# One 2-byte tile per slot of a fused feed-forward stage, turned by a transposing transfer and not by TensorE

## What is computed

```
x = x + tanh(g_xattn[0]) * L0_xattn(layernorm(x), ctx, Wq, Wk, Wv, Wo)
x = x + tanh(g_ffn[0]) * L0_ffn(layernorm(x), weight_scales, weight_q)      # bf16 x bf16
x = x + tanh(g_xattn[1]) * L1_xattn(layernorm(x), ctx, Wq, bq, Wk, bk)
x = x + tanh(g_ffn[1]) * L1_ffn(layernorm(x), W, b, A, B, gate_w, gate_b)

def L0_ffn(x, scales, q):
    w = dequantize(q, scales).astype(bfloat16)
    return einsum('bsi,oi->bso', x.astype(bfloat16), w)
```

## Time and profile before

| | |
|---|---|
| time, median of 3 runs | 1989.47 us (1989.45 to 1989.71) |
| the profiled execution's own time | 1992.98 us |
| its span, from the first to the last instruction | 1991.2 us |
| PE busy | 1956.6 us (98%) |
| DVE, ACT, POOL busy | 1037.7, 742.4, 724.0 us |
| TensorE clock granted, mean | 0.993 of full speed |
| HBM traffic | 177.01 MB read, 57.94 MB written, 118 GB/s |

### The profile page before, as it was taken

One profiled execution on the slowest core, in us unless ns is written; L12 is line 12 of the kernel. 1 busy time (PEld: TensorE's weight loads), 2 busy tenths in 40 slices (PEclk: granted clock), 3 DMA queues, 4 the chain that ended last, 5 costly groups with the idle time before them and its releaser, 6 DMA issues.

```text
span 1991.2 us, 37538 instructions
## 1 busy us (share of the span) xinstructions
PE 1956.6 (98%) x14016; PEld 1298.5 (65%) x14030; DVE 1037.7 (52%) x2012; ACT 742.4 (37%) x1560; POOL 724.0 (36%) x719
## 2 busy tenths in 40 slices
PE   8999999999999999999999999999999999999998
PEld 3488888885666666666666655667566676666665
DVE  5655545534555555555555663434334345656554
ACT  5421111222555555555555661111111224444441
POOL 0000000111565566565555550101101246666662
PEclk9999999999999999999999999999999999999999
DMA  7433333333222222223322444433333485665661
GB/s 249 132 99 109 96 109 100 121 97 81 67 69 68 66 69 66 66 69 81 98 72 66 115 121 140 116 92 115 114 113 111 141 274 166 208 214 185 210 208 58
DMA packets 317583, 236.43 MB, mean 119 GB/s; under 512 B 248270, under 2 KB 285134, under 8 KB 313004
## 3 DMA queue, kind: packets, MB, share of 16 engines
q1 hardware_dynamic: 290364, 222.47, 38.3%
q10 hardware_dynamic: 27120, 12.60, 2.4%
HBM read 177.01 MB, written 57.94 MB: 118 GB/s over the span
## 4 chain that ended last, share of the span: by engine, by line
PE 88%; DVE 3%; ACT 2%; DMA 1%; issue 1%; POOL 0%; SPq 0%; DVEq 0%; ACTq 0%
PE a_pr L723 14%; PE b_kv_ps L1137 9%; PE b_kv_ps L1141 9%; PE c_x_ps L1609 9%; PE d_f_ps L2050 8%; PE b_s_ps L1178 8%; PE b_o_ps L1193 7%; PE c_t_ps L1630 7%; PE d_a_ps L1835 3%; PE a_pr L719 3%; PE b_mx_ps L1153 3%; PE c_f_ps L1662 2%; PE d_s_ps L1803 2%; DMA t_scratch<-c_tT 1%; PE c_x_ps L1204 1%; DVE d_y3T L2005 1%
## 5 line engine op out<-in xcount | busy, mean ns | idle before, releaser
L937 POOL TENSOR_TENSOR b_probT<-b_exp,b_probT 128x448 f16<-128x448 f32 (+2 forms) x256 | 265.3, 1038 | 297.2 <-ACT b_probT L1001 297.1
L503 POOL TENSOR_TENSOR cT<-ctx_raw,cT 128x375 f16<-128x375 f32 x256 | 222.4, 888 | 134.6 <-ACT cT L498 133.6
L723 PE MATMUL a_pr<-a_yT,proj_q_p 128*128 128x256 f16 x2016 | 223.2, 273 | 0.0
L723 PEld LDWEIGHTS a_pr<-a_yT,proj_q_p 128*128 128x128 f16 x2016 | 197.3, 98 | 23.4
L1141 PE MATMUL b_kv_ps<-wkv_p,cT 128*128 128x384 f16 (+1 forms) x1152 | 210.6, 325 | 0.0
L1071 DVE TENSOR_REDUCE b_nmax<-b_mx_ps 112x2 f16<-112x974 f32 x128 | 149.6, 1169 | 109.6 <-PE b_mx_ps L1153 109.5
L1137 PE MATMUL b_kv_ps<-cT,wkv_p 128*128 128x375 f16 x1152 | 198.9, 323 | 0.0
L1178 PE MATMUL b_s_ps<-b_qT,b_kT 96*128 96x448 f16 (+5 forms) x768 | 190.6, 356 | 2.2 <-DMA b_qT<-b_nrow 2.2
L1193 PE MATMUL b_o_ps<-b_probT,b_v 128*128 128x448 f16 (+5 forms) x768 | 187.3, 351 | 0.0
L999 ACT ACTIVATE b_exp<-b_s_ps 128x448 f32<-128x448 f32 (+2 forms) x256 | 137.7, 538 | 129.7 <-PE b_s_ps L1178 124.4
L2050 PE MATMUL d_f_ps<-wo_early,d_y3T 128*112 128x512 f16 x768 | 175.7, 382 | 0.0
(11 more groups left out here) (209 smaller groups left out, 2797.8 us busy)
## 6 DMA issues: line engine op xcount, KB each, us to landing
ctx_raw<-in_ctx_t SPq DMA_DIRECT2D x32, 1500.0 KB, 7.4
d_cn_raw<-in_ctx_nat SPq DMA_DIRECT2D x32, 512.0 KB
b_qT<-qk_scratch SPq DMA_DIRECT2D x32, 336.0 KB, 4.1
o_scratch<-b_o SPq DMA_DIRECT2D x128, 84.0 KB, 2.0
qk_scratch<-a_heads SPq DMA_DIRECT2D x70, 144.0 KB, 2.1
d_cn_raw<-in_ctx_nat SPq DMA_DIRECT2D x16, 476.0 KB
x_scratch<-c_x SPq DMA_DIRECT2D x14, 512.5 KB, 3.5
tiles_in<-in_x SPq DMA_DIRECT2D x14, 512.0 KB, 4.0
```

Of the source, the lines that this page charges most:

```text
L503: pool.tensor_tensor(cT[:, p, 1, k, 0:S], ctx_raw[:, k, :], cT[:, p, 0, k, 0:S], ALU.subtract).then_inc(split_lo, 1)
L723: last = mm(pr[:, n % PR, 0:GT * P], w[:, b, k, at * P:(at + 1) * P], yT[:, g % 2, a, k, :], start=(x == 0 and k == 0), stop=(x == 2 and k ...
L937: pool.tensor_tensor(pT[0:m, c, 1, :], ex[0:m, i % 2, :], pT[0:m, c, 0, :], ALU.subtract).then_inc(p_lo, 1)
```

## The change

Turning `y1` leaves TensorE. SP issues one transposing transfer per tile, SBUF to SBUF, from `y1` to `y1T`. PE's eight transposes and ACT's copy are gone; PE waits for the transfer before the feed-forward product, and DVE waits for the transfer of the tile before, where it waited for PE's transposes. SP's wait and issue (`turn_y1`) stand at the start of slot s, ahead of `load`, for tile s-1. SP's slots are all written out, none is in a loop; the other engines keep their loops.

```diff
+                    def turn_y1(t):
+
+                        sp.wait_ge(y1_ready, t + 1)
+                        wait(sp, f_done, 2 * t)
+                        sp.dma_start(y1T.rearrange("p (k r) -> p k r", k=KD), y1[:, :], transpose=True
+                                     ).then_inc(y1_turned, 16)
+
                     def slot(j, p, s):
+                        if inside(s - 1, TILES):
+                            turn_y1(s - 1)
                         if inside(s, TILES) and inside(s + 1, TILES) and not (isinstance(s, int) and s == 0):
                             load(j + p, 1 - p, s + 1)
...
-                    run_slots(sp, slot, SLOTS, 4)
+                    for s in range(SLOTS):
+                        slot(s // 2, s % 2, s)
...
-                        if inside(s - 1, TILES):
-                            act.wait_ge(y1tr, s)
-                            act.activation(y1T[:, :], tr[:, 0, :].bitcast(BF16), ACT.Copy).then_inc(y1T_ready, 1)
...
                         if inside(s, TILES):
-                            wait(dve, y1tr, s)
+                            wait(dve, y1_turned, 16 * s)
                             norm1_scaled(dve, y1[:, :], x1[:, p, :], P, s).then_inc(y1_ready, 1)
...
-                        if inside(s - 1, TILES):
-                            pe.wait_ge(y1_ready, s)
-                            for k in range(KD):
-                                last = pe.transpose(tr[:, 0, k * P:(k + 1) * P].bitcast(BF16), y1[:, k * P:(k + 1) * P],
-                                                    identb[:, :])
-                            last.then_inc(y1tr, 1)
...
                         if inside(s - 1, TILES):
-                            pe.wait_ge(y1T_ready, s)
+                            pe.wait_ge(y1_turned, 16 * s)
```

More of the change, by code:

```diff
@@ L1357, in build @@
                 wo_done, x1_ready = sem("c_wo_done"), sem("c_x1_ready")
-                y1_ready, y1tr, y1T_ready = sem("c_y1_ready"), sem("c_y1tr"), sem("c_y1T_ready")
+                y1_ready, y1_turned = sem("c_y1_ready"), sem("c_y1_turned")
                 f_done, f_read, x2_ready = sem("c_f_done"), sem("c_f_read"), sem("c_x2_ready")
```

## The result

The changed kernel takes 2009.35 us, the median of three runs (2004.42 to 2009.95), against 1989.47 us before. The ratio is 1.0093, with a 95% interval of 1.0079 to 1.0107: slower by 0.9%. The profiled execution took 2009.35 us with a span of 2007.6 us, 16.4 us more than the 1991.2 of before. The forecast was 2007.5 us, and +18.0 us on the span.

A forecast was written before the change was run, and what follows sets the result against it. PE, busy for 98% of the span, was taken to bound the kernel. The terms -5.4 + 2.2 + 0.5 + 24.9 - 7.2 + 3.0 = +18.0 us on 1989.5 gave 2007.5 us, range 1999 to 2026 us.

The forecast's parts named there:

- Steady slots: Slots 2 to 13 of stage c: PE is freed of 0.45 us of transposes in each, 5.4 us gained.
- The transfer's price: Time of one transposing transfer in a steady slot, taken as 5 us, within 13.9 us of room.
- The 18.6 us of the other row: High bound for one transposing transfer, from the dearest row per KB, 84 KB in 6.1 us.
- Slot 1: First tile: the transfer lands behind the 2 MB feed-forward weight, so the product starts late, 2.2 us lost.
- Slot 13: The raw context is issued later and lands 6 to 8 us later, mostly covered by POOL's idle time; 0.5 us lost.
- Slot 14: Last tile: the transfer lands behind some 7 MB of stage d loads and PE stands; 24.9 us lost.
- The bound of 20.2 us: Low bound of the loss in slot 14, with the landing at 1629.9, where 512 KB report after 9.5 us.
- What comes back: Turn to stage d: PE's earlier 4.46 us wait and 2.70 us of slow clock go away, 7.2 us gained.
- The new fall of the clock: PE's clock drops after its new 25 us stall in slot 14; 3.0 us lost, bounds 1.5 and 5.
- That the transfer passes the loads: Rival: it lands within about 3 us of issue at the end and costs nothing there or in slot 1; 1983.2 us, chance 0.08.
- That it is slow by itself: Rival: the transfer takes over 13.9 us and decides every slot; at 18 us, 2089 us; chance 0.12.

The follow-up runs named there:

- e3: The changed kernel, but tiles 0 and 13 are turned on PE and copied by ACT as before; 1984.79 us, in a second run 1982.79 us.
- e2: The changed kernel, but tile 13 alone is turned on PE and copied by ACT as before; 1987.84 us, ratio to before 0.9989.
- e8: The changed kernel measured again with nothing edited; 2008.07 us, ratio to before 1.0096.
- e7: The changed kernel, but SP issues the transfer of tile 13 ahead of the last 2 MB load, behind 5.5 MB; 2001.12 us.
- e1: The kernel before the change, with SP's slots of stage c written out and nothing else changed; 1989.26 us, ratio 0.9998.
- e4: The changed kernel, but SP issues the transfer of tile 13 ahead of all nine loads for stage d; 1993.66 us, ratio to before 1.0012.
- e9: e3 with the store of `c_tT` issued first in slot 14, ahead of biases, rows and raw context; 1979.12 us, ratio to before 0.9944.

## Why the prediction was right, and where its terms were off

- **Steady slots, 5.4 us gained: right.** Eleven slots give 4.91 us, and with that of slot 2 it is 5.4. `e3` shows it as a time, 5.6 and 8.7 us under the kernel before in its two runs.
- **The transfer's price, 5 us: too high, the row was right.** It lands after 3.2 us, exactly what the store of the same size took in the earlier trace rows. The 18.6 us of the other row were far off. So was the estimate of 10.5 us from the Trainium skill's 1309 ns for a block ("VectorE: DVE Perf Modes", section The three transpose paths): eight blocks take 3.2 us, with all that goes before and after. The rule of the Trainium skill that a transposing transfer is as fast as an ordinary one ("Advanced Engine Details and Errata", section X-Bar Transpose (TRN2)) held for an idle queue.
- **Slot 1, 2.2 us lost: a term was missing.** The product starts 1.53 us later, but PE's clock fell as well, 1.7 us more, so the slot cost 3.2 us (`e2` against `e3`: 3.1 us). I had counted the clock in slot 14 alone. In `e8` PE waited 3.05 us and not 3.82, and the product ran at full speed; in `e7`, after 3.14 us, it took 5.31 us.
- **Slot 13, 0.5 us lost: nothing was lost.** POOL's split started at 1582.18 and not 1576.74, and its idle time covered that. The slot is 30.95 us like the others.
- **Slot 14, 24.9 us lost: right in mechanism, 3.8 us too large.** It was 21.1. The step that was off is the landing of the last load. I took 27.6 us after issue from the earlier trace rows, but in that execution some 3 MB were issued behind it from 1620.03 on. In the changed kernel the next issue, the store of the rows that the late product makes, comes at 1641.93, and the load landed after 23.7 us. The other runs agree: where the 3 MB followed while it was in flight it took 27.2 us (`e1`), 27.6 (`e2`), 26.8 and 26.3 (`e3`, its two runs), 26.3 (`e4`) and 25.9 (`e9`), and where only the transposing transfer followed 24.7 (`e8`). So what is issued behind a load can delay it; the order in the queue is not a strict one. The distance behind it, 1.5 us forecast, was 0.9. The bound of 20.2 us, taken from the 512 KB that reported early, was the closer one.
- **What comes back, 7.2 us: 5.9.** The 4.46 us came back in full and the clock with them, but the first sequence of stage d took 23.0 us and not 21.7, held by POOL and DVE (see `e9`).
- **The new fall of the clock, 3.0 us: 2.6.**
- **The sum.** The forecast of +18.0 stands against +16.4 in the profiled executions and +19.9 in the medians. The second measurement of the change, `e8`, is 18.3 us over the kernel before beside it. The median came close partly by luck: I laid the 18.0 on a median 3.5 us under its own profiled execution, and after the change the two are the same. The forecast of the span, too, was closer than its terms deserve: 3.8 us too much in slot 14, 0.5 in slot 13 and 0.4 for the clock, against 1.0 too little in slot 1, 1.3 too much in what came back, and 0.7 at the end of the span that no term had.
- **The rivals.** That the transfer passes the loads was refuted by the 0.9 us between the two landings, and from the other side by `e4`. That it is slow by itself was refuted by the median landing of 3.2 us, and in slot 14 by the 3.6 us of `e4`.

## What to carry to other kernels

A step that leaves a busy engine for a transfer gains what it cost there only where the transfer lands before its reader wants it. In a steady slot it took 3.2 us of 13.9; at the last tile only 3.9 us lay between `y1` and the product (1605.93 to 1609.84), and 7.5 MB stood ahead. Look at each place where large loads are issued at about that time, here the first and the last tile of fourteen, and leave the step on the engine there. In one queue a small transfer landed with what the issuing program had put ahead of it, and another engine's queue did not help it here, with its small packets beside large ones. A wait that an engine had for a small store behind large loads goes away by issuing the store first; here that gave 4.4 us in the trace on top of the 5.4 of the steady slots.

## What the runs showed that I had not expected

- Two queues shared the 16 DMA engines packet for packet while both had packets waiting, 213 to 213 and 83 to 84 in 4 us each; the one stretch of 75 to 366 is where most engines seem to have run out of loads. A transposing transfer of 256 KB goes out in about 1054 packets of 250 bytes; next to loads with packets of up to 16 KB it took 31.2 us on a queue of its own, and 24.0 and 24.7 us behind them in the same queue.
- Issuing a transfer behind large loads holds the issuing engine: SP was held for 16.90 us by one instruction that takes 1.26 us otherwise, and ACT for 1.49 us on a queue of its own.
- PE's clock after a wait: after 3.82 us of standing, the next 4.93 us were granted 0.65 of full speed; after a wait of 3.05 us in `e8` the product took no longer than at full clock. The length of the wait alone does not decide it: in the second run of `e3`, `d_ag_ps` took 2.45 us after a wait of 2.78, where it takes 1.62 at full clock. After 21.57 us of standing it was not worse than after 4.46: 2.6 us lost there, 2.7 in the earlier trace rows.
